# Eight products of a layer pass as four of 32 rows, new orders on four engines, and one-row products as 128 rows

## What is computed

```
qkv = shift(x) @ Wqkv                      # 16 heads of 64
q, k = rotary(l2norm(q)), rotary(l2norm(k))
out = softmax(8 * q k^T, window of 32 and the window before) v
x = x + out @ Wo
x = x + (a * gelu(gate)) @ W2 + b2         # hg = layernorm(shift(x)) @ W1 + b1
```

## Time and profile before

| | us |
|---|---|
| median of three runs | 4423.32 (4418.15 to 4425.26) |
| the profiled execution | 4414.45 |
| its span, first to last instruction | 4412.6 |
| PE busy in the span | 3968.6 (90%) |
| DVE busy | 3577.9 (81%) |
| ACT busy | 2960.0 (67%) |
| POOL busy | 2218.5 (50%) |
| cross attention | 0 to 310 |
| layers | 310 to 3557 |
| the rest | 3557 to 4413 |

### The profile page before, as it was taken

The page is one execution under the profiler, slowest core; times in us unless marked ns, Lnnn a source line. Parts: engine busy times, 40 slices in busy tenths (PEclk is TensorE's granted clock), DMA queues, the critical chain, the costliest instruction groups (busy, mean ns, idle before and its releaser), DMA issues. The chain is left out here.

```text
span 4412.6 us, 117906 instructions
## 1 busy us (share of the span) xinstructions
PE 3968.6 (90%) x43247; PEld 2389.2 (54%) x43247; DVE 3577.9 (81%) x8501; ACT 2960.0 (67%) x5496; POOL 2218.5 (50%) x1398
## 2 busy tenths in 40 slices
PE   8989999999999999999999999999999854737735
PEld 5645555555555555555555555555555533525534
DVE  7878999899998999989999899989999756466341
ACT  3437778778777778778778778778778655636302
POOL 1016666666666666666666666666666400130006
PEclk9999999999999999999999999999999966868558
DMA  3002223323223323233223332232322200000102
GB/s 103 1 2 66 65 66 69 82 65 70 65 64 87 70 63 68 65 84 71 66 63 68 83 71 66 65 91 65 70 66 66 53 1 13 1 0 14 67 8 37
DMA packets 187147, 249.17 MB, mean 56 GB/s; under 512 B 88660, under 2 KB 129110, under 8 KB 186326
## 3 DMA queue, kind: packets, MB, share of 16 engines
q1 hardware_dynamic: 181078, 238.37, 23.0%
q0 software_dynamic: 5632, 4.33, 0.8%
HBM read 39.55 MB, written 14.30 MB: 12 GB/s over the span
## 5 line engine op out<-in xcount | busy, mean ns | idle before, releaser
L1446 POOL TENSOR_TENSOR f_rot_a<-f_rot_a,f_rot_b 128x1024 f32<-128x1024 f32 x384 | 908.3, 2371 | 302.5 <-DVE f_rot_b L1180 197.2
L1454 POOL TENSOR_TENSOR f_rot_a<-f_rot_a,f_norm 128x1024 f32<-128x1024 f32 x384 | 731.3, 1904 | 648.0 <-DVE f_norm L1198 524.6
L874 PE MATMUL f_bank<-f_w_vo,f_xs_t 128*32 128x512 f32 x6144 | 815.8, 603 | 0.2
L1177 DVE TENSOR_TENSOR f_rot_a<-f_bank,f_rot 128x512 f32<-128x512 f32 x768 | 523.3, 682 | 66.8 <-ACT f_squares L1541 32.5
L1550 ACT ACTIVATE f_vo<-f_bank 128x512 f32<-128x512 f32 x768 | 458.7, 597 | 170.9 <-PE f_bank L874 163.2
L1541 ACT ACTIVATE f_squares<-f_bank 128x512 f32<-128x512 f32 x768 | 455.9, 594 | 116.3 <-PE f_bank L860 68.8
L1564 ACT ACTIVATE f_k_t<-f_bank 64x512 f32<-64x512 f32 x768 | 452.7, 589 | 104.0 <-PE f_bank L896 99.5
L1180 DVE TENSOR_TENSOR f_rot_b<-f_bank,f_rot 128x512 f32<-128x512 f32 x768 | 505.9, 674 | 0.0
L1460 POOL TENSOR_TENSOR f_prob<-f_score,f_stat 128x512 f32<-128x512 f32 x384 | 400.5, 1043 | 188.4 <-DVE f_stat L1230 187.8
L1184 DVE TENSOR_REDUCE f_sums<-f_squares 128x16 f32<-128x1024 f32 x384 | 464.6, 1210 | 4.6 <-ACT f_squares L1541 4.6
L906 PEld LDWEIGHTS f_bank<-f_k_t,f_q_t 128*32 128x32 f32 x12288 | 345.3, 110 | 179.5 <-issue 100.2
(11 more groups left out here) (459 smaller groups left out, 7380.8 us busy)
## 6 DMA issues: line engine op xcount, KB each, us to landing
f_vo_off<-f_vo SPq DMA_DIRECT2D x1152, 128.0 KB, 2.3
f_vo_off<-f_vo SPq DMA_DIRECT2D x384, 64.0 KB, 2.1
f_vo_dram<-f_vo_pair SPq DMA_DIRECT2D x48, 128.0 KB, 1.8
f_x_shifted<-s_all SPq DMA_DIRECT2D x48, 128.0 KB
f_x_shifted<-s_all SPq DMA_DIRECT2D x48, 127.0 KB
f_w_qk<-in_Wqk SPq DMA_DIRECT2D x10, 512.0 KB, 4.3
f_w_vo<-f_vo_dram SPq DMA_DIRECT2D x10, 512.0 KB, 4.8
e_w<-in_e_W SPq DMA_DIRECT2D x2, 2048.0 KB, 9.9
```

Of the source, the lines that this page charges most:

```text
L874: done = nc.tensor.matmul(bank[V][32 * w:32 * w + 32, :], x[:, at:at + 32], w_vo[:, 4 * g:4 * g + 4, w // 2, :], start=True, stop=True)
L1177: nc.vector.tensor_tensor(rot_a[:, slot, n, :].rearrange("p (h d) -> p h d", h=GROUP), source, c_tab, ALU.mult)
L1446: nc.gpsimd.tensor_tensor(rot_a[:, slot, :, :], rot_a[:, slot, :, :], rot_b[:, g, :, :], ALU.add).then_inc(rot_summed, 1)
L1454: nc.gpsimd.tensor_tensor(heads, heads, over(norm[:, 16 * g:16 * g + 16], [128, 16, HEAD_DIM]), ALU.mult).then_inc(qk_normed, 1)
```

## The change

In the layers three helpers get an argument `rows`. With it a product of 128 output rows becomes four of 32 rows, each with its own 32 columns of the left operand and its own 32 partitions of the bank, and the semaphore counts up with the last.

```diff
+            def multiply(to, left, right, rows):
+
+                size = 32 if rows else left.shape[1]
+                for at in range(0, left.shape[1], size):
+                    part = slice(at, at + size)
+                    done = nc.tensor.matmul(to[part, :], left[:, part], right, start=True, stop=True)
+                return done
...
-                nc.tensor.matmul(flat(K), chunk_x(t), w_qk[:, 1, 512 * g:512 * g + 512], start=True, stop=True).then_inc(k_done, 1)
+                multiply(flat(K), chunk_x(t), w_qk[:, 1, 512 * g:512 * g + 512], rows).then_inc(k_done, 1)
```

The last block runs on into the first of the next pass. DVE's list of a pass in the first third, as far as the prediction speaks of it (`rotate(p, t, g, n, part)`, n = 1 is k):

```diff
+                if live(p, 0):
+                    rotate(p, 0, 1, 0, 0)
+                    rotate(p, 0, 1, 0, 1)
+                    inverse_lengths(p, 0)
                 if live(p, -1):
                     total(p, -1, 0)
...
+                    rotate(p, 1, 0, 1, 0)
                 if live(p, -1):
                     invert(0)
                 if live(p, 1):
+                    rotate(p, 1, 0, 1, 1)
+                    rotate(p, 1, 0, 0, 0)
+                if has(p, 2):
+                    normalise(p - 2, 0)
+                if live(p, 1):
+                    rotate(p, 1, 0, 0, 1)
                 if live(p, -1):
                     highest(p, -1, 1)
                 if has(p, 2):
                     normalise(p - 2, 1)
+                if live(p, -2):
+                    residual(p, -2)
                 if has(p, 3):
                     store(p - 3)
...
                 if live(p, -1):
                     total(p, -1, 1)
+                    invert(1)
+                if live(p, 1):
                     rotate(p, 1, 1, 1, 0)
                     rotate(p, 1, 1, 1, 1)
+                    length(p, 1, 0)
                     length(p, 1, 1)
                 if live(p, 0):
                     highest(p, 0, 0)
                 if live(p, 1):
                     inverse_lengths(p, 1)
```

```diff
-                nc.tensor.matmul(to[:, :], ones_b[:, :], mask_b[:, 2 * p + b, :].unsqueeze(1).broadcast_to([1, GROUP, CTX]), start=True, stop=False)
+                nc.tensor.matmul(to[:, :], ones_b[:, :], mask_b[:, 2 * p + b, :].unsqueeze(1).broadcast_to([128, GROUP, CTX]), start=True, stop=False)
...
-                    last = nc.tensor.matmul(s, ones[:, :], bs[:, :], start=False, stop=True)
+                    last = nc.tensor.matmul(s, ones[:, :], bias_rows[:, :], start=False, stop=True)
```

More of the change, by code:

```diff
@@ L980, in down_proj @@
                     for k, n in enumerate((128, 128, ONES_ROW + 1)):
-                        done = nc.tensor.matmul(bank[F][:, 128 * t:128 * t + 128], gate[0:n, k, 128 * t:128 * t + 128], w_2[0:n, k, :],
-                                                start=(k == 0), stop=(k == 2))
+                        for at in range(0, 128, 32 if rows else 128):
+                            size = 32 if rows else 128
+                            done = nc.tensor.matmul(bank[F][at:at + size, 128 * t:128 * t + 128], gate[0:n, k, 128 * t + at:128 * t + at + size], w_2[0:n, k, :],
+                                                    start=(k == 0), stop=(k == 2))
                 done.then_inc(f_done, 1)
@@ L1070, in body @@
                     turn_k(p, 1, 0)
+                    values_a(p, 1, 1)
+                if live(p, -1):
+                    mix(p, -1, 1)
+                if live(p, 2):
+                    project_q(p, 2, 1, rows=True)
+                if live(p, 1):
+                    scores(p, 1, 0)
+                if live(p, 3):
+                    project_k(p, 3, 0, rows=True)
+                if live(p, 1):
+                    turn_q(p, 1, 1)
                 if live(p, 0):
@@ L1282, in body @@
                     rotate(p, 0, 0, 1, 0)
+                    rotate(p, 0, 0, 1, 1)
+                if has(p, 3):
+                    hide(p - 3, 2)
+                if live(p, -2):
+                    total(p, -2, 1)
+                if live(p, 0):
                     rotate(p, 0, 0, 0, 0)
-                    rotate(p, 0, 0, 1, 1)
+                    rotate(p, 0, 0, 0, 1)
+                    length(p, 0, 0)
+                    rotate(p, 0, 1, 1, 0)
                 if live(p, -2):
@@ L1287, in body @@
                 if live(p, 0):
-                    rotate(p, 0, 0, 0, 1)
-                    length(p, 0, 0)
-                if has(p, 3):
-                    hide(p - 3, 2)
+                    rotate(p, 0, 1, 1, 1)
                 if live(p, -1):
@@ L1380, in body @@
                 if live(p, 3):
+                    rotate(p, 3, 0, 1, 1)
+                if has(p, 1):
+                    statistics(p - 1)
+                if live(p, 3):
                     rotate(p, 3, 0, 0, 0)
                     rotate(p, 3, 0, 0, 1)
+                    length(p, 3, 0)
+                if has(p, 2):
+                    hide(p - 2, 0)
                 if live(p, 1):
@@ L1402, in body @@
                     inverse_lengths(p, 3)
-                    rotate(p, 3, 1, 0, 1)
-                    rotate(p, 3, 1, 1, 1)
+                if has(p, 2):
+                    hide(p - 2, 1)
+                if live(p, 2):
+                    highest(p, 2, 1)
                 if has(p, 1):
@@ L1478, in body @@
                 if live(p, 0):
+                    add_up(p, 0, 1)
                     scale(p, 0, 1)
+                if has(p, -1):
+                    take_x(0, p + 1)
                 if live(p, 1):
@@ L1664, in body @@
                     seed(p, 0, 1)
-                    exponential(p, 0, 0)
-                if has(p, 2):
-                    take_gate(p - 2, 0)
+                    copy_k(p, 0, 1)
                 if live(p, 1):
@@ L1671, in body @@
                     copy_prob(p, -1, 1)
+                if has(p, 2):
+                    take_gate(p - 2, 0)
+                if live(p, 0):
+                    exponential(p, 0, 0)
+                if live(p, 2):
+                    square(p, 2, 0, 0)
                 if live(p, 1):
+                    copy_values(p, 1, 0, 1)
                     copy_q(p, 1, 0)
                 if live(p, 2):
-                    square(p, 2, 0, 0)
+                    square(p, 2, 1, 1)
+                if live(p, 1):
+                    seed(p, 1, 0)
+                    copy_k(p, 1, 0)
+                if has(p, 2):
+                    take_gate(p - 2, 1)
                 if live(p, 0):
```

385 lines of the change are left out of this document (178 added, 207 removed).

## The result

The kernel after takes 4455.3 us (median of 4 runs, 4450.0 to 4455.7), the one before 4423.4 (4418.2 to 4425.3): ratio 1.0070, 95% interval 1.0056 to 1.0083. It is 32 us slower; 40 us faster was forecast, and the time lies above the range. The profiled execution has a span of 4453.1 us (before 4412.6).

What follows compares the result with a forecast made beforehand. PE's list was taken to bound the layers. Layers -26, cross attention -5 and routing -9 gave -40 us off the median of 4423.32: 4383 us, range 4330 to 4415.

Steps and rivals of the forecast that it cites:

- The price of the blocks: PE's list in a settled layer pass: 11 tiled blocks instead of 16 save 1.48 us, from 65.87 to 64.3.
- Rival 4: Layer products in four parts pay for their weight loads, 7 us a pass: 4687 us; chance 0.02.
- The lock of DVE on POOL: In layer passes, a DVE normalising or root step waits for the running POOL instruction; 3.4 us a pass before.
- steps (a) to (c): DVE in a layer pass: roots' 1.9 us wait goes; normalise's halves wait for POOL until 5.3 and 9.9 after the roots.
- the first stall: PE waits 0.4 us at project_k(2, 0) in each layer pass, because DVE frees bank K late.
- My estimate of DVE's list: All DVE steps of a settled layer pass without any waiting: 59 us, leaving 5 us.
- rival 2: Roots of t = 0 still fall into POOL's add_up, 2.0 us more on DVE: about 67 a pass, 4459; chance 0.10.
- Later in the pass DVE has 4 us of waits for PE, and catches up: After 1.0 us of PE waiting, DVE adds no further delay in the layer pass: 65.3 us a pass.
- Layer boundaries I leave unchanged: No change where layers meet, +-3 us; the K product waiting for weights costs 5 times 0.5 us at most.
- Filling and draining: The layers' passes without all four lists full: left unchanged, within the same +-3 us as the boundaries.
- Cross attention: One-row products taken as 128 rows save about 25 us of PE, but DVE is as late: 5 us (0 to 12).
- Routing: Eight products at 0.36 us instead of 0.52 save 1.3 us in each of 6 to 8 passes: 9 us (6 to 11).

Runs made afterwards that it cites:

- the list free of the three stalls: Kernel after with normalise behind length(1, 0), boundary loads ahead of the copies of values, and the 127-row transfer as 112 and 15: 4324.0 us, 0.9780 of before.
- The experiment on normalise: Kernel after with both halves of normalise moved behind length(1, 0), where POOL is idle or in a short weigh: ratio 0.9930 to the kernel before.
- the one-row products only: Kernel before with only the one-row products of cross attention and routing taken as 128 rows: 4408.1 us against 4417.4, ratio 0.9980.

## Why the prediction was wrong

**The price of the blocks: right.** 64.3 was forecast for PE's list without stalls (64.28 by the same prices, kept to hundredths); the list free of the three stalls takes 64.64, 0.20 of it a small stall. The old order with four parts came to 66.87 where the prices gave 66.70, and the difference between whole and four parts to 1.53 where they gave 1.52. Rival 4 is out: by it eight tiled products would have cost 7 us a pass, and inside a block one takes 0.86, as a whole one does between whole ones. So the rule of the Trainium skill that the prediction set beside it ("TensorE: Matmul & The Clock Gate", section "The mechanism") does not hold as it stands for column tiles of the same rows here. The same section also lets a load into the background weight buffer go ahead of a running product; whether that is what happens here no run shows.

**The lock of DVE on POOL, steps (a) to (c): right.** The two halves end 5.4 and 10.2 us after the roots (5.3 and 9.9), the first stall is 0.93 (0.4 forecast) and both are 1.21 (1.0). The experiment on normalise shows the cause. My estimate of DVE's list was high: its terms add up to 58.1, not to the 59 that I wrote, and DVE is busy for 57.3 us once the waits for POOL are gone. The price of rival 2 rests on it.

**"Later in the pass DVE has 4 us of waits for PE, and catches up": wrong.** This is the step that failed. I priced DVE's steps and not the transfers that its list waits for. `statistics` had moved ahead of the rotate of q(3, 0), and x lands only 10 us after residual(-1), because one of its transfers goes piece by piece, at the share of one DMA engine. DVE waits 1.12 us for it and PE 0.67; with 0.2 in small stalls and 0.2 more than forecast at the first two the pass is 66.36 and not 65.3: 45 x 1.06 = 48 us of the error of 72, 30 of them from this wait. In the profile before, nothing waits for that transfer in a settled pass, so no row named it. But SP's queue was held for 6.46 us behind it there too, and the distance from issue to landing of each transfer that a moved step waits for had to be read. The Trainium skill has the rule that would have named it ("DMA: Bandwidth & Descriptors", section "Why a DMA increments its semaphore by 16 and not by 1": a transfer is spread over the largest number up to 16 that divides its outermost dimension, for 127 partitions one). The trace agrees: a share of 0.09, one piece of 256 bytes every 14 ns, and 112 rows are not held.

**"Layer boundaries I leave unchanged": wrong by 25 us.** The second step that failed. I gave 0.5 us to the K product that waits for its weights. The pass that it heads grows by 2.7 us a boundary: PE idles 3.3 us on average in place of 1.75, and the clock is at 0.50 behind that at all five boundaries, where before it was at two. The transpose that no longer stands ahead of the product is 0.5 us of the longer wait, as I had it. The rest lies with the load itself: at four of the boundaries a copy of values ahead of it is held in SP's queue for 0.9 to 1.3 us longer than before, and at the first boundary the product starts 5.1 us after the issue in place of 4.1. With four parts in the old orders the wait is as long (17.3 us over the five, 16.4 after, 8.7 before), so the new order is not needed for it. The other part, 2.2 us a boundary, is DVE, whose first rotate of tile 1 now stands earlier than the table's second half lands (4.4 us of waiting in place of 1.9); that one belongs to the new order, for the second pass doesn't grow in the old one. A step that waits for a transfer had to be costed with the transfer's landing, and with the clock behind the wait, not as a swap of two steps. Why SP's queue holds the copy stays open.

**Filling and draining**, also left unchanged: -9 and +6 (4 us of the latter and of the earlier first fold are only the place of `fold` in the list). The runs place both with the new orders: folds 0 to 3 take 193 us with the one-row products only and 195 with four parts in the old orders, but 179 to 184 in every kernel with the new ones. From the last `fold` to the start of the last down projection it is 122 us in both of the former, 128 in the kernel after, and 117 where the 127 rows alone are split. What in the orders shortens the filling no run shows.

**Cross attention: right** (5 forecast, 5.7 measured). **Routing: half** (9 forecast, 4.8 measured, under its own range of 6 to 11). The term mis-sized is the price of a product behind another of the same kind: I took 0.36 from the first one after the transposes, it is 0.43. Eight of them then save some 0.7 us a pass and not 1.3.

Rival 2 names the right sign with the wrong mechanism: the roots do not fall into `add_up`, and their first step takes 0.17 us. No rival held a wait for a transfer.

## What to carry to other kernels

When steps are put in another order, write down for each moved step every semaphore that it waits for, transfers included, and when that is given; a wait that never showed in the profile because it had slack is the one that will surprise. A list with little slack has no room for a foreign wait: the same slow transfer cost nothing before and 0.67 us a pass after. And treat the places where weights are reloaded as their own case, with the clock that falls behind an idle stretch.

## What the runs showed of the hardware

- A transfer of 127 rows (127 KB) went one piece of 256 bytes after the other, every 14 ns, at a DMA share of 0.09, some 7 us in all, and what SP issued behind it was held in the queue: 6.5 us for 0.5 KB, or 5.1 for a copy that otherwise takes 0.6. With 112 and 15 rows no issue of x was held for more than 0.97.
- Behind 2.9 to 3.6 us of idle time at the five boundaries of the kernel after PE ran at 0.50 each time, at the one shown for 6 us; there the clock cost nearly as much as the wait. Before, idle for 1.7 to 1.8, it ran at 0.50 behind two of the five (from 1368 to 1370, for one) and at 1.00 behind the others.
- DVE's normalising steps waited for POOL's instructions one by one: 5.67 us for four steps beside a full POOL, 1.14 where POOL had only the last 0.3 us of a `weigh`.
- A product in four parts of 32 columns costs what a whole one does (0.86 us start to start, at 512 columns and f32); only the changes of kind count (1.53 us a pass for the eight, 1.52 by the prices).
